# The mixer's depthwise convolution moved to GpSimd: tokens on partitions, neighbours fetched by shifted copies, nothing of it on TensorE

## The reference

```
x = x + 0.5 * ffn(layernorm(x))
x = x + mixer(layernorm(x))
x = x + 0.5 * ffn(layernorm(x))
```

```
t   = conv1d over the sequence, kernel 3, zero padding 1, one filter per channel, + conv_b
u, v = x Wu^T + bu, x Wv^T + bv
gates = sigmoid(relu(x Wg1^T + bg1) Wg2^T + bg2)
mixer = t + (cumsum(u * gates over the sequence) * (v * gates)) Wu
```

## Time and profile before

| | |
|---|---|
| median of 3 runs | 1098.14 us (1097.51 to 1098.58) |
| the profiled execution, its own time | 1099.39 us |
| its span | 1097.6 us |
| busy: TensorE, VectorE, ScalarE, GpSimd | 1050.2, 721.0, 543.9, 147.6 us |
| mixer: from the first product to the last of `times_wu` | about 467 to 654 us |

### The profile page before, as it was taken

How to read it: one execution, slowest core, us unless ns; L and a number is a source line. 1 busy time by engine, 2 the same in 40 slices (tenths; PEclk the granted TensorE clock), 3 DMA queues, 4 the chain that set the end, 5 groups by cost and what they waited for, 6 DMA issues and landing times.

```text
span 1097.6 us, 20918 instructions
## 1 busy us (share of the span) xinstructions
PE 1050.2 (96%) x7912; PEld 994.6 (91%) x7912; DVE 721.0 (66%) x1089; ACT 543.9 (50%) x851; POOL 147.6 (13%) x135
## 2 busy tenths in 40 slices
PE   8699999999999999599999996999999999999995
PEld 6699999999999999478777776999999999999995
DVE  7556566666577777378686875557767677665552
ACT  4445454655556575254333234455666656554431
POOL 2201111113020210100000022002112031130101
PEclk9699999999999999899999996999999999999998
DMA  8377636466455651400011235336566565654410
GB/s 308 132 273 275 218 127 232 177 225 220 171 205 191 244 180 73 166 12 1 1 39 39 77 112 182 133 136 244 184 231 226 191 244 181 229 209 145 168 39 24
DMA packets 83277, 177.33 MB, mean 162 GB/s; under 512 B 4192, under 2 KB 4704, under 8 KB 83168
## 3 DMA queue, kind: packets, MB, share of 16 engines
q1 hardware_dynamic: 75488, 152.61, 39.3%
q0 software_dynamic: 7168, 23.07, 5.9%
q10 hardware_dynamic: 576, 1.05, 0.3%
HBM read 162.04 MB, written 18.87 MB: 165 GB/s over the span
## 4 chain that ended last, share of the span: by engine, by line
PE 94%; DVE 1%; DMA 1%; ACT 1%; issue 1%; POOL 1%; POOLq 0%; ACTq 0%; SPq 0%; DVEq 0%
PE psH L1217 13%; PE psH L1218 13%; PE psH L1219 13%; PE acc L1225 12%; PE acc L1224 12%; PE acc L1226 12%; PE acc L1217 3%; PE acc L1219 3%; PE acc L1218 3%; PE psT L1272 1%; PE psT L1433 1%; PE psH L1345 1%; PE acc L1389 1%; PE psH L1389 1%; PE psT L1538 1%
## 5 line engine op out<-in xcount | busy, mean ns | idle before, releaser
L1217 PE MATMUL psH<-dth,wih 128*128 128x240 f32 (+5 forms) x1024 | 294.1, 287 | 0.0
L1225 PE MATMUL acc<-htl,woh 128*128 128x240 f32 (+5 forms) x1024 | 293.1, 286 | 0.0
L1218 PE MATMUL psH<-dtl,wih 128*128 128x240 f32 (+5 forms) x1024 | 293.1, 286 | 0.0
L1226 PE MATMUL acc<-hth,wol 128*128 128x240 f32 (+5 forms) x1024 | 292.9, 286 | 0.0
L1219 PE MATMUL psH<-dth,wil 128*128 128x240 f32 (+5 forms) x1024 | 292.9, 286 | 0.0
L1224 PE MATMUL acc<-hth,woh 128*128 128x240 f32 (+5 forms) x1024 | 292.8, 286 | 0.0
L791 DVE TENSOR_TENSOR wol<-raw_wo,woh 128x1024 fp32r<-128x1024 f32 x128 | 155.6, 1223 | 146.4 <-ACT woh L608 146.4
L642 ACT ACTIVATE gel<-psH 128x320 f32<-128x320 f32 x256 | 112.0, 437 | 187.8 <-PE psH L1219 182.6
L608 ACT ACTIVATE woh<-raw_wo 128x1024 fp32r<-128x1024 f32 x128 | 134.2, 1056 | 132.0 <-PE acc L1226 131.9
L1217 PEld LDWEIGHTS psH<-dth,wih 128*128 128x128 f32 x1024 | 193.4, 189 | 0.4
L1218 PEld LDWEIGHTS psH<-dtl,wih 128*128 128x128 f32 x1024 | 193.4, 189 | 0.0
(11 more groups left out here) (194 smaller groups left out, 1162.4 us busy)
## 6 DMA issues: line engine op xcount, KB each, us to landing
raw_wi<-in_wi SPq DMA_DIRECT2D x64, 1024.0 KB, 5.1
raw_wo<-in_wo SPq DMA_DIRECT2D x64, 1024.0 KB, 5.4
out_x<-xt SPq DMA_DIRECT2D x4, 1024.0 KB, 5.8
xt<-in_x SPq DMA_DIRECT2D x6, 512.0 KB, 8.1
xt<-x SPq DMA_DIRECT2D x3, 1024.0 KB, 9.9
raw_u<-in_wuT SPq DMA_DIRECT2D x1, 1024.0 KB, 10.9
raw_u<-in_wvT SPq DMA_DIRECT2D x1, 1024.0 KB, 12.5
xt<-in_x ACTq DMA_DIRECT2D x2, 256.0 KB, 3.4
```

What stands on the lines that cost most here:

```text
L1217: pe.matmul(out, lh, rh, start=first, stop=False)
L1218: pe.matmul(out, lh, rl, start=False, stop=False)
L1225: pe.matmul(out, lh, rl, start=False, stop=False, skip_group_check=True)
L1226: return pe.matmul(out, ll, rh, start=False, stop=False, skip_group_check=True)
```

## The change

The convolution keeps the layout of the norm: a token per partition. The token before and the token after are then one partition away, and SyncE fetches them by transfers within SBUF.

- `xn` shrinks to two groups (tile t lies at t mod 8) and new buffers `late` and `soon` of one group each hold the rows of the token before and after. `xT` shrinks to one group, since no tap reaches over its edge.
- SyncE's `shift(g)` fills `late` by transfers over 112 and over 15 partitions, and by one for the token that comes from the tile before (partition 127 to partition 0); likewise `soon`. The row that crosses from the first to the second group of a sequence is held in `held_row` (the place of `lgT`), and in the other direction goes straight to `soon`. `shift(0)` to `shift(2)` stand ahead of `keep(0)`, `shift(3)` between `keep(0)` and `keep(1)`.
- The filters and the bias must lie along the row and be the same on all partitions: TensorE turns 16 columns, spread over 128, into the four `acc` banks, and ScalarE copies them to `conv_row`. This is done once, between layer one and the mixer.
- GpSimd's `convolve(g)` makes, for each tile, three products and the sums, seven tensor_tensor instructions of 128x512, and adds the result to `xt` itself. The powers of the next groups are put between the tiles. The second layer's powers follow all four groups.
- Gone: `conv_mid`, `tap`, `turn_conv`, and VectorE's first addition in `adds`.
- New waits: the norm of group g >= 2 waits for conv_added of group g - 2; ScalarE's first `copy_logits` of layer two waits for all transfers to `late`; SyncE loads the second layer's first weights after all of `conv_added`; the powers of group 2 and 3 stand behind the waits at the head of `convolve(1)` and `convolve(2)`.

```diff
-        xn = put("xn", [P, TILES, D], F32)
+        xn = put("xn", [P, 2 * GROUP, D], F32)
+        late = put("late", [P, GROUP, D], F32)
+        soon = put("soon", [P, GROUP, D], F32)
...
+                    def shift(g):
+                        this = group_of(g)
+                        sp.wait_ge(n_xn, g + 1)
+                        if g == 0:
+                            sp.wait_ge(n_xn0, 1)
+                        if g % 2:
+                            sp.dma_start(soon[P - 1:P, GROUP - 1, :], this[0:1, 0, :]).then_inc(soon_edge, 16)
+                        sp.wait_ge(late_free, g + 1)
+                        for a, z in ((0, P - 16), (P - 16, P - 1)):
+                            sp.dma_start(late[a + 1:z + 1, :, :], this[a:z, :, :]).then_inc(late_in, 16)
+                        sp.dma_start(late[0:1, 1:GROUP, :], this[P - 1:P, 0:GROUP - 1, :]).then_inc(late_in, 16)
+                        if g % 2:
+                            sp.wait_ge(row_held, 16 * (g // 2 + 1))
+                            sp.dma_start(late[0:1, 0, :], held_row).then_inc(late_in, 16)
+                        else:
+                            sp.dma_start(held_row, this[P - 1:P, GROUP - 1, :]).then_inc(row_held, 16)
+                        sp.wait_ge(soon_free, g + 1)
+                        for a, z in ((0, P - 16), (P - 16, P - 1)):
+                            sp.dma_start(soon[a:z, :, :], this[a + 1:z + 1, :, :]).then_inc(soon_in, 16)
+                        sp.dma_start(soon[P - 1:P, 0:GROUP - 1, :], this[0:1, 1:GROUP, :]).then_inc(soon_in, 16)
+
+                    shift(0)
+                    shift(1)
+                    shift(2)
                     keep(0)
+                    shift(3)
                     keep(1)
-                    sp.wait_ge(d_conv, DC * GROUPS)
+                    sp.wait_ge(n_xTl, DC * GROUPS)
+                    sp.wait_ge(conv_added, TILES)
...
+            def convolve(g):
+                this = group_of(g)
+                def by_row(k):
+                    return conv_row[:, k, :]
+                if g == 0:
+                    pool.wait_ge(rows_spread, 4)
+                pool.wait_ge(late_in, 16 * (3 * (g + 1) + (g + 1) // 2))
+                pool.wait_ge(soon_in, 48 * (g + 1))
+                pool.wait_ge(row_held, 16 * (g // 2 + 1))
+                pool.wait_ge(n_T, DC * (g + 1))
+                for j in range(GROUP):
+                    t = GROUP * g + j
+                    if g % 2 == 0 and j == 1:
+                        power(g + 1, slice((g + 1) * GROUP, (g + 2) * GROUP), n_var, n_rstd)
+                    if g == 1 and j == 0:
+                        power(g + 1, slice((g + 1) * GROUP, (g + 2) * GROUP), n_var, n_rstd)
+                    if g % 2 == 0 and j == GROUP - 1:
+                        pool.wait_ge(soon_edge, 16 * (g // 2 + 1))
+                    pool.tensor_tensor(this[:, j, :], this[:, j, :], by_row(1), ALU.mult).then_inc(conv_step, 1)
+                    pool.tensor_tensor(late[:, j, :], late[:, j, :], by_row(0), ALU.mult).then_inc(late_scaled, 1)
+                    pool.tensor_tensor(soon[:, j, :], soon[:, j, :], by_row(2), ALU.mult).then_inc(soon_scaled, 1)
+                    pool.wait_ge(conv_step, 4 * t + 1)
+                    pool.tensor_tensor(this[:, j, :], this[:, j, :], by_row(3), ALU.add).then_inc(conv_step, 1)
+                    pool.wait_ge(conv_step, 4 * t + 2)
+                    pool.wait_ge(late_scaled, t + 1)
+                    pool.tensor_tensor(this[:, j, :], this[:, j, :], late[:, j, :], ALU.add).then_inc(conv_step, 1)
+                    pool.wait_ge(conv_step, 4 * t + 3)
+                    pool.wait_ge(soon_scaled, t + 1)
+                    pool.tensor_tensor(this[:, j, :], this[:, j, :], soon[:, j, :], ALU.add).then_inc(conv_step, 1)
+                    pool.wait_ge(conv_step, 4 * t + 4)
+                    if j == GROUP - 1:
+                        if g % 2:
+                            pool.memset(late[0:1, 0, :], 0.0).then_inc(late_free, 1)
+                            pool.sem_inc(soon_free, 1)
+                        else:
+                            pool.sem_inc(late_free, 1)
+                            pool.memset(soon[:, GROUP - 1, :], 0.0).then_inc(soon_free, 1)
+                    pool.tensor_tensor(xt[:, t, :], xt[:, t, :], this[:, j, :], ALU.add).then_inc(conv_added, 1)
...
+                    power(0, slice(0, GROUP), n_var, n_rstd)
+                    pool.memset(late[0:1, 0, :], 0.0).then_inc(late_free, 1)
+                    pool.sem_inc(soon_free, 1)
                     for g in range(GROUPS):
-                        power(g, slice(g * GROUP, (g + 1) * GROUP), n_var, n_rstd)
+                        convolve(g)
...
                     act.wait_ge(rstd_sem, 2 * (g + 1))
+                    if g >= 2:
+                        act.wait_ge(conv_added, GROUP * (g - 1))
...
+                    act.wait_ge(late_in, 224)
                     copy_logits(0)
...
                 def adds(w):
-                    dve.wait_ge(p_conv, w + 1)
-                    dve.tensor_tensor(xt[:, w, :], psT[w % 2][:, :], xt[:, w, :], ALU.add).then_inc(d_addc, 1)
+                    dve.wait_ge(conv_added, w + 1)
                     dve.wait_ge(p_uv, w + 1)
-                    dve.wait_ge(d_addc, w + 1)
                     dve.tensor_tensor(xt[:, w, :], psH[w % 2][:, :], xt[:, w, :], ALU.add).then_inc(d_addu, 1)
```

More of the change, by code:

```diff
@@ L176, in build_kernel @@
         top[0] = shared
-        xT = put("xT", [P, DC, SEQ + 2], F32)
+        xT = put("xT", [P, DC, GT], F32)
+        conv_row = put("conv_row", [P, 4, D], F32)
         glh = put("glh", [P, 2, DC, GT], F32R)
@@ L292, in build_kernel @@
         n_xT = sem("n_xT")
-        n_pad = sem("n_pad")
+        rows_turned = sem("rows_turned")
+        rows_spread = sem("rows_spread")
+        late_free = sem("late_free")
+        late_in = sem("late_in")
+        soon_free = sem("soon_free")
+        soon_in = sem("soon_in")
+        soon_edge = sem("soon_edge")
+        row_held = sem("row_held")
+        conv_step = sem("conv_step")
+        conv_added = sem("conv_added")
+        late_scaled = sem("late_scaled")
+        soon_scaled = sem("soon_scaled")
         n_xTh = sem("n_xTh")
@@ L714, in take_xT @@
                             round_xT(g, c)
-                def conv_mid(g):
-                    for c in range(DC):
-                        act.activation(convT(g, c), xT[:, c, place(g):place(g) + GT], ACT.Identity,
-                                       bias=small[:, CB0 + c:CB0 + c + 1],
-                                       scale=small[:, CW0 + 3 * c + 1:CW0 + 3 * c + 2]).then_inc(a_conv, 1)
                 def relu(g):
@@ L737, in _ @@
                 x1_tiles = x1[0:T, :].rearrange("(n p) d -> p n d", p=P)
+                act.wait_ge(s.wi_lo, STEPS * E)
+                for k in range(4):
+                    act.wait_ge(rows_turned, k + 1)
+                    act.activation(conv_row[:, k, :], acc[k][:, :], copy).then_inc(rows_spread, 1)
                 act.wait_ge(uv_lo, 2 * DC)
@@ L756, in _ @@
                             glob_hi(i - 1)
-                        if c == 0:
-                            conv_mid(g)
-                            if not more:
-                                copy_tiles(0, nxt)
+                        if c == 0 and not more:
+                            copy_tiles(0, nxt)
                         if c == 1:
@@ L1148, in chain @@
                     dve.tensor_tensor(vg[c % 2][:, :], vg[c % 2][:, :], ug[:, :], ALU.mult).then_inc(d_glob, 1)
-                def tap(g, k):
-                    q = column(g) + k - 1
-                    if k == 0:
-                        dve.wait_ge(n_pad, 2)
-                    else:
-                        dve.wait_ge(n_xT, DC * (g + 2 - g % 2))
-                    for c in range(DC):
-                        dve.wait_ge(d_tap if k else a_conv, DC * g + c + 1)
-                        dve.scalar_tensor_tensor(
-                            convT(g, c), xT[:, c, q:q + GT],
-                            small[:, CW0 + 3 * c + k:CW0 + 3 * c + k + 1], convT(g, c),
-                            ALU.mult, ALU.add).then_inc(d_conv if k else d_tap, 1)
                 def next_stats(w):
@@ L1177, in _ @@
                             moments(g + 1, n_var, [x1_in[g]] * GROUP)
-                        if c == 1:
-                            tap(g, 0)
                         if c == 2:
@@ L1185, in _ @@
                                     next_stats(w)
-                            if not more:
-                                tap(g, 2)
-                        if c == 3 and more:
-                            tap(g, 2)
                 glob_lo(DC * GROUPS - 1)
@@ L1574, in _ @@
                 nxt = layers[1]
+                pe.wait_ge(s.eoT_done, DC * (E + 1))
+                for k in range(4):
+                    for c in range(DC):
```

(4 more changed lines are left out.)

47 lines of the change are left out of this document (13 added, 34 removed).

## The result

The changed kernel takes 1138.87 us (median of 3 runs, 1136.59 to 1140.53) against 1098.14 us: a ratio of 1.0362, 95% interval [1.0344, 1.0381], or 40.7 us more. The prediction was 1129 us in a range of 1106 to 1158. Its profiled execution took 1138.87 us around a span of 1137.1, 39.5 us more than the span before.

A forecast was written before the change was run, and what follows sets the result against it. TensorE bounds the mixer before, GpSimd after: 475 + 127.0 + 0.5 + 3 x 1.3 + 25.5 + 42.5 = 674. The last add then ends at 685.8, not 654.41: 31 us on the 1098.14 median, 1129 us, range 1106 to 1158.

The forecast's parts named there:

- TensorE's 7 us: Mixer, TensorE: sixteen blocks of four transposes are removed, 0.44 us each, 7.0 us in all.
- GpSimd's end: End of GpSimd's last convolution in the mixer: at 674 us, ending last and deciding the time.
- 16 tiles: Mixer, GpSimd: seven operations a tile at 1.10 us plus 0.24, 7.94 us a tile; four convolutions take 127 us.
- turns with VectorE: Mixer: GpSimd and VectorE's two-SBUF-input instructions block each other whole instruction by whole instruction, costing GpSimd 42.5 us.
- three gaps: Between convolutions: GpSimd stands still for each next group's shifts, 8.5 us a gap, 25.5 in all, bounds 6 and 12.
- TensorE's stall: Before group 3's turning: TensorE idles for the norm behind GpSimd's late power, 24.4 us late, but doesn't end last.
- Behind GpSimd's end: After convolution 3: layer two's power, VectorE's L858, TensorE's tiles 14 and 15; last add ends at 685.8 against 654.41.
- The tail: After the last add: 13 us to the first gather unchanged, 31 us later; later first expert weights lose nothing.
- A: Mixer: turns cost GpSimd nothing, TensorE decides; -4 us, 1094; chance 0.07.
- B: Mixer: turns cost GpSimd half, or its operations take 0.93 us; -21 or -19 us, 1108 to 1110; chance 0.22.
- C: Mixer: GpSimd slower, 1.29 us an operation (1150) or 1.43 (1166); gaps of 12 us add 11; chance 0.19.
- D: Whole kernel: the change does nothing, TensorE's 7 us less cancelled by waits, GpSimd ending at about 643; chance 0.03.

The follow-up runs named there:

- kernel with three operations a tile: Changed kernel without the products and sums of the side taps, so three of seven GpSimd operations a tile are left: 1093.28 us, ratio 0.9953.
- small kernel: Separate kernel, nothing of the reference: phases of twelve 128x512 instructions on GpSimd, VectorE or both; GpSimd's product 1.22 us alone, 1.59 beside VectorE's.
- kernel without reads: Changed kernel with 14 GpSimd memsets a tile in place of the seven operations, convolution left out: 1114.99 us, ratio 1.0154.
- powers put first: Changed kernel with the powers of groups 2 and 3 ahead of the waits in convolve(1) and convolve(2): 1137.84 us, ratio 1.0354.
- six-operation kernel: Changed kernel with shifts tile by tile, powers of group 3 and layer two early, bias added by VectorE: 1125.51 us, ratio 1.0247.
- reordering: Kept rows written ahead of weight loads, on the changed kernel with tile-by-tile shifts, early powers and bias on GpSimd: 1114.54 us, ratio 1.0145.

## Why the prediction was right, and where its terms were off

The direction, the mechanism and the bound were right. The number, 1129, was 10 us too low. I go by the prediction's steps.

**TensorE's 7 us.** Not seen in the changed kernel, where TensorE waits. The kernel with three operations a tile fits it: there GpSimd is no bound, the time is 5 us below before, and the first gather is 7.4 us earlier by distance, against the 7 for 16 blocks.

**GpSimd's end: 674 forecast, 681.8 measured.** The terms:

| term | forecast | measured | how |
|---|---|---|---|
| start of convolution 0 | 475 | 475.8 | timeline; see below |
| 16 tiles | 127.0 | 142.4 | 16 x 8.90 |
| turns with VectorE | 42.5 | 29.8 | remainder, below |
| three gaps | 25.5 | 28.0 | 9.18 + 9.60 + 9.22 |
| powers and edges | 4.4 | 5.8 | 3 x 1.26 + 4 x 0.5 |

The start agrees by luck: in this execution the mixer began 2.4 us earlier than in that of the kernel before, and the shift came some 3 us later than my way of reckoning gives. I had two transfers follow the loads of `x1` at full rate, with a latency of 1.7 us that no run shows; SyncE in fact issued the pieces from 461.65 to 469.48, and the last of them took 7.9 us to land.

The four convolutions span 46.3, 45.9, 43.5 and 42.3 us, together 178.0; less tiles, powers and edges, 29.8 are left for the turns. **Two terms were mis-sized, with opposite signs.** The operation: I took 1.10 us between 0.93 and 1.29; it is 1.22, so the bound from the small products' slope was the near one and the spreads misled. They repeat one operand, and the small kernel puts such an operation at 1.00 us (12.02 / 12). Two sizes measured here, 1.22 at 512 elements and 2.30 at 1024, give 2.11 ns an element and a fixed 0.14 us. By the Trainium skill (GPSIMD Engine Reference, "Performance versus the Vector engine") the estimate was 1.12; the trace has 1.22, and the difference is about the fixed part, which scaling its time for 2048 elements down to 512 nearly drops.

The turn: I charged GpSimd VectorE's whole instruction less 0.08 us. In the small kernel a turn costs it 0.37 for a product and 0.88 for a scan. With my count of 47 products and low parts and 16 scans, that is 17.4 + 14.1 = 31.5 us, and seven eighths of it 27.6, near the 29.8 measured; the step of 1.71 in the mixer (a loss of 0.49 beside 0.37) goes some way to the rest. The kernel without reads gives 29.4 by another way. So the turns are there, and their price was overstated by 40%. The signs that the prediction named are in the trace: a step of 1.7 next to VectorE, a scan far above 1.28, three gaps of which transfers end at least two, and VectorE's L928 (L858 before) waiting for GpSimd. Two signs were off: TensorE stood idle 18.1 us and not 24 before the last turning, and 2.8 and not 6 before tile 14, there at the full clock. The Trainium skill (SBUF — State Buffer, "Who interferes with whom") names the reads as what is shared, and the kernel with memsets agrees: 682 ns for VectorE's low part beside GpSimd's writes, 1161 beside its reads.

**The gaps.** Forecast 8.5 between 6 and 12 us; measured 9.2 to 9.6. Two shifts of 896 KB land 5.4 and 5.3 us after issue, and SyncE's queue in the second gap shows what sets the length (the changed kernel's timeline):

```profile
575.65 1.39 SPq L388 DMA_DIRECT2D late<-xn  x2
...
580.21 1.46 SPq L397 DMA_DIRECT2D soon<-xn  x2
581.71 1.77 SPq L398 DMA_DIRECT2D soon<-xn  x1
```

I had charged the second transfer 2.7 us for its bytes. Here it is issued 4.6 us after the first, since the pieces of `late` take that long to issue, and the last piece 6.1 us after the first; GpSimd starts at 586.76, 5.1 us behind it. In the third gap the pieces are issued with the same spacing (628.38, 632.95, 634.45), and GpSimd starts 5.0 us behind the last, so a transfer very likely ends that one too.

**TensorE's stall.** Forecast: 24.4 us late at the turning of group 3, and not deciding. Measured: 599.99 against 569.63, 30.4 late, and not deciding, which the powers put first show.

**Behind GpSimd's end.** Forecast 11.4 us (685.8 less 674.4) to the last addition's end, measured 692.80 - 681.77 = 11.0. The sum was right and one part of it wrong. The changed kernel's timeline there:

```profile
684.04 0.26 DVE L928 TENSOR_TENSOR sel<-sel,facts 128x96 f32<-128x96 f32 x1 [5.35 <-POOL facts L492]
684.22 0.68 DVE L1184 TENSOR_TENSOR xt<-psH,xt 128x512 f32<-128x512 f32 x1
684.96 0.50 PE L1262 MATMUL psH<-wuh,glh 128*128 128x512 f32 x1 [2.82 <-DVE xt L1184]
688.77 2.11 DVE L962 TENSOR_TENSOR at_lane<-lanes,t 128x512 f32<-128x512 f32 x2
692.13 0.67 DVE L1184 TENSOR_TENSOR xt<-psH,xt 128x512 f32<-128x512 f32 x1
```

VectorE does wait for layer two's power (5.35 us), and tile 14 waits for add 12. But TensorE, later than I had it, was idle for only 2.8 us and did tile 14 at full clock, 2.8 us in place of 5.0. What I didn't have is VectorE's own delay: the two lanes ran beside GpSimd's spread and took 2.11 us for 1.33.

**The tail.** "13 us to the first gather" was 11.6 (692.80 to 704.35). From the gather to the end of the span it is 432.8 us where it was 430.2: "nothing is lost" there was off by 2.5. The weights come later in the changed kernel and the kept rows with them; which of it makes the 2.5 us I didn't separate.

**The account of the 9.7 us missed** (1138.87 against 1098.14 + 31). GpSimd's end is 7.4 late against the forecast (681.8 against the 674.4 of its terms), the part to the last addition -0.4, the part to the gather -1.4, what is behind it +2.5, the rounding of 31.4 to 31 +0.4; that makes 8.5 of span. The profiled execution of before was 1.25 us above its median and that of after at its median, which is the rest.

**The rivals.** A (turns cost nothing) fell: 29.8 us of turns. B had two halves; turns at 70% of my price went its way, the operation went the other. C had the operation right in direction: 1.22 is nearly two thirds of the way from 1.10 to its 1.29. D fell. That the number came as near as it did is partly luck: the two errors nearly cancel, and either alone would have moved it by 13 to 15 us.

## What to carry to other kernels

Before work goes to an idle GpSimd, add up three things for the stretch in question and not for the kernel: the operations at their measured price, each encounter with a VectorE instruction that has two SBUF inputs, and the gaps for its inputs. Here a tile of seven operations cost 8.9 us alone, where TensorE's share of a tile was 43.7 / 4 = 10.9, and it was the turns and gaps, 58 us together, that pushed it over. Look also at how long the transfers take to issue: with many small pieces that, and not the bytes, set the length of the gap here.

A repair on the bounding engine that adds a two-input instruction to VectorE is paid for on both, as the six-operation kernel shows. And once a stretch ends earlier, look at what was just hidden behind it: here a queue of weight loads in front of rows that the next layer needs held the gather up for 8.5 us, of which the reordering gave 2.6 back in the time.

## What the hardware showed that I had not expected

- GpSimd's multiplication by a constant, one input, took 36.05 / 24 = 1.50 us at 128x512, more than the 1.22 us of a product of two inputs; in the second half of those rows VectorE's products ran beside it in 9.69 us for twelve, 0.81 each.
- A VectorE cast and a GpSimd memset, neither of which has two inputs, slow each other: 8.98 and 8.68 us for twelve, 0.75 and 0.72 each. Beside VectorE's two-input products a memset takes 0.47 (5.66 us for twelve), and a cast of the hidden layer, also 128x512 and SBUF to SBUF, took 0.42 in the kernel before, with GpSimd idle.
- VectorE loses more than GpSimd in such pairs: its product went from 0.61 (7.32 us for twelve beside memsets) to 1.58 us (18.99 / 12), GpSimd's from 1.22 to 1.59.
